# A pre-norm decoder layer on one core: the first tile prepared in halves, three loads reordered, and the loop's pieces placed anew

## What is computed

```python
x = x + self_attention(layernorm(x), Wq, Wk, Wv, Wo)   # 32 heads, 8 key/value heads of 16, RoPE, causal
x = x + cross_attention(layernorm(x), ctx, Wq, bq, Wk, bk)  # softmax((xWq+bq)(ctxWk+bk)^T / sqrt(512)) ctx
h = layernorm(x)                                       # FFN with weights rounded to -1, 0, 1 times a scale
x = x + ((h @ gate.T) * (h @ up.T)) @ down.T           # inner width 1376
```

## Time and profile before

| | us |
|---|---|
| median of 3 runs (226.37 to 226.87) | 226.63 |
| the profiled execution, its own time | 226.21 |
| its span, first to last instruction | 224.5 |
| PE busy in it | 209.5 |
| DVE, ACT, POOL busy in it | 146.9, 124.6, 65.8 |

### The profile page before, as it was taken

The page is one execution under the profiler, slowest core; times in us unless marked ns, Lnnn a source line. Parts: engine busy times, 40 slices in busy tenths (PEclk is TensorE's granted clock), DMA queues, the critical chain, the costliest instruction groups (busy, mean ns, idle before and its releaser), DMA issues.

```text
span 224.5 us, 4343 instructions
## 1 busy us (share of the span) xinstructions
PE 209.5 (93%) x1500; PEld 152.0 (68%) x1500; DVE 146.9 (65%) x556; ACT 124.6 (56%) x210; POOL 65.8 (29%) x87
## 2 busy tenths in 40 slices
PE   8899999999897899998999997999999999999993
PEld 3389878677664675565945445788887877767771
DVE  2488677967889875998424589886645665343333
ACT  2748788777988346197767917357325033323220
POOL 4599917794223383152202212000000010000000
PEclk9999999999999999999999999999999999999999
DMA  6999500024612210649000640000000000020002
GB/s 176 377 402 411 196 1 1 7 72 183 237 65 61 84 49 13 178 134 309 20 4 0 205 170 0 3 0 3 0 0 1 3 0 3 0 93 3 0 0 95
DMA packets 9078, 19.98 MB, mean 89 GB/s; under 512 B 1152, under 2 KB 1536, under 8 KB 9056
## 3 DMA queue, kind: packets, MB, share of 16 engines
q1 hardware_dynamic: 8480, 19.60, 25.2%
q10 hardware_dynamic: 576, 0.10, 0.2%
HBM read 18.58 MB, written 1.05 MB: 87 GB/s over the span
## 4 chain that ended last, share of the span: by engine, by line
PE 77%; DVE 7%; ACT 6%; issue 5%; DMA 3%; SPq 1%; DVEq 0%; POOL 0%; ACTq 0%
PE ps L1376 17%; PE ps L1230 13%; PE ps L1391 8%; PE ps L1267 5%; PE ps L1298 3%; PE ps L1329 3%; PE ps L1210 3%; PE ps L1439 3%; DMA wqkv<-wqkv_dram 3%; PE ps L1164 3%; PE ps L1521 3%; PE ps L1450 2%; PE ps L1480 2%; PE ps L1179 2%; PE ps L1189 2%
## 5 line engine op out<-in xcount | busy, mean ns | idle before, releaser
L1044 DVE CUSTOM_DVE_ANT_0 ps<-ps,maskf 128x128 f32<-128x128 f32 (+1 forms) x128 | 41.2, 394 | 3.4 <-PE ps L1450 2.1
L584 POOL TENSOR_SCALAR_AFFINE_SELECT prob<-prob 128x512 f32<-128x512 f32 x32 | 19.8, 642 | 49.0 <-ACT prob L802 49.0
L802 ACT ACTIVATE prob<-ps 128x1536 f32<-128x1536 f32 x16 | 23.3, 1455 | 19.4 <-PE ps L1486 19.4
L503 POOL TENSOR_TENSOR rstd<-veps,neghalf 128x1 f32<-128x1 f32 x12 | 7.3, 609 | 57.7 <-DVE veps L837 57.7
L672 ACT CAST in_hi<-inter 128x256 f16<-128x256 f32 (+1 forms) x22 | 8.9, 405 | 23.1 <-DVE inter L997 23.1
L1376 PE MATMUL ps<-h_hi,gate_q 128*128 128x256 f16 (+1 forms) x88 | 20.4, 273 | 0.0
L1376 PE MATMUL ps<-h_lo,up_q 128*128 128x256 f16 (+1 forms) x88 | 20.4, 273 | 0.0
L1376 PE MATMUL ps<-h_lo,gate_q 128*128 128x256 f16 (+1 forms) x88 | 20.4, 273 | 0.0
L1376 PE MATMUL ps<-h_hi,up_q 128*128 128x256 f16 (+1 forms) x88 | 20.4, 272 | 0.0
L997 DVE TENSOR_TENSOR inter<-gate_s,ps 128x256 f32<-128x256 f32 (+1 forms) x22 | 9.2, 419 | 15.6 <-PE ps L1376 14.7
L665 ACT ACTIVATE gate_s<-ps 128x256 f32<-128x256 f32 (+1 forms) x22 | 8.4, 384 | 18.8 <-PE ps L1376 18.8
(11 more groups left out here) (189 smaller groups left out, 539.2 us busy)
## 6 DMA issues: line engine op xcount, KB each, us to landing
raw<-gate_dram SPq DMA_DIRECT2D x1, 2752.0 KB, 17.1
raw<-up_dram SPq DMA_DIRECT2D x4, 688.0 KB, 4.1
wqkv<-wqkv_dram SPq DMA_DIRECT2D x4, 384.0 KB, 5.8
raw<-down_dram SPq DMA_DIRECT2D x2, 768.0 KB, 5.2
x<-x_dram SPq DMA_DIRECT2D x4, 256.0 KB, 5.2
xwq<-xwq_dram SPq DMA_DIRECT2D x1, 1024.0 KB, 8.9
xwk<-xwk_dram SPq DMA_DIRECT2D x1, 1024.0 KB, 11.1
wo<-wo_dram SPq DMA_DIRECT2D x1, 1024.0 KB, 18.2
```

Of the source, the lines that this page charges most:

```text
L584: nc.gpsimd.affine_select(out=v, in_=v, compare_op=ALU.is_ge, fill=0.0, base=0, pattern=[[0, GROUP], [1, P]], channel_multiplier=-1).then_ ...
L802: nc.scalar.activation(prob[:, i % 2, :], ps[:, 3:6, :].rearrange("p a b -> p (a b)"), ACT.Exp, scale=DH ** -0.5).then_inc(exp_done, 1)
L1044: nc.vector.tensor_tensor_reduce(scores, scores, mask, 1.0, LOWEST, ALU.add, ALU.max, to).then_inc(max_done, 1)
```

## The change

**The first tile.** DVE normalises tile 0 in two halves of 256 columns. PE transposes each half into a bank of its own (banks 0 and 6) and ACT copies each on its own. `project_first` now takes one part k of the weights and does both column ranges with it, so q, k and v of tile 0 are complete together; the transposes of tile 1 stand ahead of the last part, and ACT copies them ahead of the last high part of the weights. The DVE order of the statistics and of `tile_low(1)` is as it was.

**The first loads.** x of tile 1 is now issued behind part 1 of the weights, x of tile 2 behind part 3.

**The loop.** Many side pieces have moved by a place or a slot; the chunk (2, 1) goes from DVE to POOL; the context loads start one group later, and down load 0 is issued after group 12 in place of 10, load 1 as before.

```diff
-        TILE_BANK = (0, 5, 6, 0)
+        TILE_BANK = (None, 5, 6, 0)
+        FIRST_BANKS = (0, 6)
...
-        POOL_CHUNKS = [(0, 0), (0, 1), (0, 2), (0, 3), (1, 0), (1, 1), (1, 2), (1, 3), (2, 4)]
+        POOL_CHUNKS = [(0, 0), (0, 1), (0, 2), (0, 3), (1, 0), (1, 1), (1, 2), (1, 3), (2, 1), (2, 4)]
...
-            ([("out", 10), ("max", 13)], [("a", 3, 1), ("n2", 1), ("tern", 1, 3)], [("xT", 1, 0), ("xT", 1, 1),
-             ("high", "wo", 0)]),
-            ([("out", 11), ("max", 14), ("abs", 2, 0), ("abs", 2, 1)], [("g", 0, 0), ("g", 0, 1)], [("abs", 2, 2),
-             ("low", "wo", 0), ("abs", 2, 3)]),
...
-            ([("low", "wo", 3), ("out", 14), ("max", 17), ("n3", 0)], [("xo", 1)], [("tern", 2, 1)]),
...
+            ([("out", 10), ("max", 13)], [("a", 3, 1), ("n2", 1)], [("xT", 1, 0), ("xT", 1, 1), ("high", "wo", 0)]),
+            ([("abs", 2, 0), ("max", 14), ("abs", 2, 1), ("out", 11)], [("g", 0, 0), ("abs", 2, 2), ("g", 0, 1)],
+             [("abs", 2, 3)]),
...
+            ([("max", 17), ("out", 14), ("n3", 0), ("low", "wo", 3)], [("xo", 1)], []),
...
-        UP_LOADS, CTX_LOAD, DOWN_LOADS = {3: (0, 1), 4: (2,), 5: (3,)}, 6, {10: (0,), 12: (1,), 13: (2, 3)}
+        UP_LOADS, CTX_LOAD, DOWN_LOADS = {3: (0,), 4: (1, 2), 5: (3,)}, 7, {12: (0, 1), 13: (2, 3)}
...
             for k in range(KD):
                 sp.dma_start(wqkv[:, k, :], wqkv_d[k * P:(k + 1) * P, :]).then_inc(wqkv_in[k], 16)
-                if k < 2:
-                    load_x(1 + k)
+                if k == 1:
+                    load_x(1)
+            load_x(2)
             load_x(3)
...
+            def first_T():
+
+                for half, full, done in ((0, xnT_half_ps, xnT_half), (1, xnT_ps, xnT_sb)):
+                    act.wait_ge(full, 1)
+                    nc.scalar.copy(xnT[:, 2 * half:2 * half + 2, 0:P],
+                                   bank(FIRST_BANKS[half], T).rearrange("p (k q) -> p k q", k=2)).then_inc(done, 1)
...
-            tile_T(0)
+            first_T()
             weights_high(0)
             weights_high(1)
             normalise(1)
             weights_high(2)
+            tile_T(1)
             weights_high(3)
             normalise(2)
-            tile_T(1)
...
                 if t == 0:
-                    normalise(0, lambda: None)
+                    dve.wait_ge(rstd_ready, 1)
+                    for half, ready in ((0, xn_half), (1, xn_ready)):
+                        cols = slice(half * T, (half + 1) * T)
+                        nc.vector.tensor_scalar(xn[:, 0, cols], x[:, 0, cols], mv[:, 0, 0:1], rstd[:, 0:1],
+                                                ALU.subtract, ALU.mult).then_inc(ready, 1)
...
+            def project_first(k):
+
+                pe.wait_ge(xnT_sb if k >= 2 else xnT_half, 1)
+                pe.wait_ge(wqkv_in[k], 16)
+                for e in range(2):
+                    mm = nc.tensor.matmul(qkv_bank(0, e)[:, 0:QKV - D if e else D], xnT[:, k, 0:P],
+                                          wqkv[:, k, HEAD_COLS[e]], start=(k == 0), stop=(k == KD - 1))
+                    if k == KD - 1:
+                        mm.then_inc(qkv_ps, 1)
...
-            tile_T(0)
-            pe.wait_ge(xnT_sb, 1)
-            project_first(qkv_bank(0, 0), 0).then_inc(qkv_ps, 1)
-            tile_T(1)
-            project_first(qkv_bank(0, 1)[:, 0:QKV - D], 1).then_inc(qkv_ps, 1)
+            first_T()
+            for k in range(KD):
+                if k == KD - 1:
+                    tile_T(1)
+                project_first(k)
```

More of the change, by code:

```diff
@@ L307, in decoder_layer @@
-            ([("max", 15), ("out", 12), ("xs", 0), ("low", "wo", 1), ("low", "wo", 2), ("high", "wo", 1)],
-             [("high", "wo", 2), ("part", 2), ("abs", 2, 4)], [("xs", 1), ("xpT", 0)]),
-            ([("out", 13), ("high", "wo", 3), ("max", 16)], [("whole", 2, 0), ("whole", 2, 1)], [("xpT", 1),
-             ("xo", 0), ("tern", 2, 0)]),
-            ([("low", "wo", 3), ("out", 14), ("max", 17), ("n3", 0)], [("xo", 1)], [("tern", 2, 1)]),
-            ([("xT", 2, 0), ("out", 15), ("n3", 1), ("hl", 0), ("max", 18)], [("cc", 2), ("xT", 2, 1),
-             ("whole", 2, 2)], [("hl", 1), ("whole", 2, 3), ("whole", 2, 4), ("tern", 2, 2)]),
-        ]
@@ L315, in decoder_layer @@
[L315 to L322 removed]
+            ([("abs", 0, 1)], [("pq", 3), ("rot", 3, 0), ("st", 10)], [("abs", 0, 2)]),
@@ new lines, in decoder_layer @@
+            ([("abs", 0, 3), ("max", 0)], [("rot", 3, 1), ("pk", 3), ("st", 11), ("st", 12)], [("part", 0),
+             ("hi", 3, 0)]),
+            ([("whole", 0, 0), ("max", 1)], [], [("whole", 0, 1), ("a", 0, 0), ("whole", 0, 2)]),
+            ([("max", 2)], [("st", 13), ("tern", 0, 0)], [("a", 0, 1), ("tern", 0, 1), ("lo", 3, 0)]),
+            ([("max", 3), ("out", 0), ("st", 14)], [("hi", 3, 1)], [("a", 1, 0), ("st", 15), ("whole", 0, 3),
+             ("tern", 0, 2)]),
+            ([("out", 1), ("max", 4)], [("st", 16)], [("tern", 0, 3), ("lo", 3, 1), ("a", 1, 1), ("st", 17)]),
@@ new lines, in decoder_layer @@
+            ([("out", 2), ("max", 5)], [("st", 18)], [("abs", 1, 0), ("st", 19), ("abs", 1, 1)]),
+            ([("out", 3), ("max", 6)], [("a", 2, 0)], [("abs", 1, 2)]),
+            ([("max", 7), ("out", 4)], [], [("abs", 1, 3)]),
+            ([("out", 5), ("u", 0), ("max", 8)], [], [("u", 1)]),
+            ([("whole", 1, 0), ("out", 6), ("part", 1), ("whole", 1, 1), ("max", 9)], [], []),
+            ([("out", 7), ("whole", 1, 2), ("c",), ("max", 10)], [("cc", 0)], [("a", 2, 1)]),
+            ([("max", 11), ("cc", 1), ("out", 8)], [], [("wo", 0), ("tern", 1, 0)]),
@@ new lines, in decoder_layer @@
+            ([("out", 9), ("max", 12), ("n2", 0), ("wo", 1)], [("tern", 1, 1), ("a", 3, 0), ("whole", 1, 3)],
+             [("tern", 1, 2), ("tern", 1, 3)]),
+            ([("out", 10), ("max", 13)], [("a", 3, 1), ("n2", 1)], [("xT", 1, 0), ("xT", 1, 1), ("high", "wo", 0)]),
+            ([("abs", 2, 0), ("max", 14), ("abs", 2, 1), ("out", 11)], [("g", 0, 0), ("abs", 2, 2), ("g", 0, 1)],
+             [("abs", 2, 3)]),
+            ([("max", 15), ("out", 12), ("abs", 2, 4), ("low", "wo", 0), ("xs", 0), ("high", "wo", 1),
+             ("low", "wo", 1)], [("part", 2), ("high", "wo", 2)], [("low", "wo", 2), ("xs", 1), ("xpT", 0)]),
@@ L1168, in tile_T, with first_T @@
                 pe.wait_ge(xn_ready, t + 1)
+                if t == 2:
+                    pe.wait_ge(xnT_sb, 1)
                 if t == 3:
-                    pe.wait_ge(xnT_sb, 1)
+                    pe.wait_ge(xnT_half, 1)
                 transpose_tile(bank(TILE_BANK[t]), xn[:, t % 2, :]).then_inc(xnT_ps, 1)
             HEAD_COLS = (slice(0, D), slice(D, QKV))
-            def project_first(out, e):
-                for k in range(KD):
-                    pe.wait_ge(wqkv_in[k], 16)
-                    mm = nc.tensor.matmul(out, xnT[:, k, 0:P], wqkv[:, k, HEAD_COLS[e]],
-                                          start=(k == 0), stop=(k == KD - 1))
-                return mm
+            def first_T():
+                for half, ready, full in ((0, xn_half, xnT_half_ps), (1, xn_ready, xnT_ps)):
+                    pe.wait_ge(ready, 1)
+                    for j in range(2):
+                        k = 2 * half + j
+                        mm = nc.tensor.transpose(bank(FIRST_BANKS[half])[:, j * P:(j + 1) * P],
+                                                 xn[:, 0, k * P:(k + 1) * P], ident[:, :])
+                    mm.then_inc(full, 1)
+            def project_first(k):
[6 more added lines that the diff above has]
+                        mm.then_inc(qkv_ps, 1)
             def project_high(out, t, e):
```

39 lines of the change are left out of this document (14 added, 25 removed).

## The result

The changed kernel takes 228.45 us (median of 6 runs, 228.35 to 229.81) where the kernel before takes 226.75 beside it on the same chip: a ratio of 1.0084, with a 95% interval of 1.0064 to 1.0104, or 1.9 us. The forecast was 227.7, 1.1 us more than before. The direction held; the size is nearly twice as large by the ratio and 1.6 times by the medians (1.7 us). The median lies at the upper end of the range (228.5); the ratio, taken on the 226.63 that the prediction started from, gives 228.53, just outside it. Ratios here come from the single executions and can differ by 0.1% from the quotient of the two medians. One execution of the kernel before (727.75 us) and one of a later kernel (271.39 us, mean clock 0.756) are left out of all ratios.

The account below looks back on a forecast made before the run. PE, busy 209.5 of 224.5 us at full clock, was taken as the bound. Start +0.68, steps 15 and 16 +0.26 and step 18 +0.21 gave +1.15: 227.36, 227.8 against the median, taken as 227.7 us; range 226.2 to 228.5.

Parts of the forecast that it names:

- Its likeliest case: The whole kernel: slower at 227.7 us, from terms at the start and in the loop summing to +1.15; chance 0.53.
- step 14: In the loop: ternary chunk (1, 3) delays an exponential and one copy by 0.16 us, later copies start earlier; nothing in sum.
- start, to the first product of tile 1: Before the loop: x of tile 2 lands at 10.79, delaying DVE's low part of tile 1; +0.68 us, bounds 0.3 and 0.8.
- steps 15 and 16: In the loop: an abs chunk between two copies PE waits for, partly offset by earlier down loads; +0.26 us.
- step 17: In the loop: the prediction names no term here.
- step 18: In the loop: `wo`'s low part moves behind the normalisation, the root shortens to 0.55, the addition comes later; +0.21 us.
- rival (c): In the loop: the down loads land as late as before; +1.8 us in the whole, 228.4 us; chance 0.10.
- the first steps of the loop: Loop's first part: two exponentials pushed by 0.3 to 0.4 us, transposes change places on PE; costed at nothing.
- all that is behind the loop: After the loop: moved pieces are each ready at least 0.5 us before they are wanted; costed at nothing.
- POOL at the start: Before the loop: POOL's last two low parts of the weights run 14.8 to 18.5; costed at nothing, upper bound 0.1.
- (a): At the start: loads don't queue by bytes, x of tile 2 lands about as before; 225.9 us, chance 0.16.
- (d): At the start: PE's stall of 1.5 us brings back the slow pace, 1.3 us more; 229.0 us, chance 0.04.

Follow-up runs that it names:

- the old loads: The changed kernel with x of tiles 1 and 2 issued behind parts 0 and 1 of the weights, as before: 227.34 us, ratio 1.0042.
- the three pieces back: The kernel before with the loop's new order, except the abs chunk, ternary chunk (1, 3) and fourth low part of `wo` put back: 226.95 us, ratio 1.0010.
- the tables alone: The kernel before with only the loop's new order of side pieces, first tile and first loads as before: 227.63 us, ratio 1.0060.
- the low part first: The changed kernel, new loads kept, with DVE making the low part of tile 1 ahead of the statistics of tile 3: 229.45 us, ratio 1.0137.
- the abs chunk back: The kernel before with the loop's new order, but the down weights' third chunk summed behind both copies g, as before: 227.44 us, ratio 1.0029.
- The tables with both pieces back: The kernel before with the loop's new order, but the abs chunk and ternary chunk (1, 3) put back: 226.95 us, ratio 1.0009.

## Why the prediction was wrong

Its likeliest case was right in direction and in its mechanism for the start; it fell on its sum, +1.15 forecast and 1.9 measured, and one of its steps, step 14, was wrong outright. The terms, forecast against traces:

| | forecast | measured |
|---|---|---|
| start, to the first product of tile 1 | +0.68 | +1.2 between the means of three and five traces |
| step 14 | 0 | +0.42 to +0.44 |
| steps 15 and 16 | +0.26 | +0.57 and +0.87, both with the old loads |
| step 17 | 0 | +0.11 |
| step 18 | +0.21 | +0.16 |

In the times the new start costs 1.2 us with the old tables and 0.5 with the new, and the new tables cost 1.4 us with the old start and 0.7 with the new. Each of these is known to 0.4 to 0.7 us, so the start may have been sized right. For the loop (+0.47 forecast) the traces are clear: 1.28 us with the old start.

**Step 14** is the step that failed outright: "Nothing in sum". It cost 0.43 us. I followed the ternary chunk on ACT, where the first copy came 0.22 us later (0.16 forecast) and the next ones sooner. I didn't follow the exponential's other reader: its mask on POOL, 1.0 us later, falls on the normalisation on DVE, and that takes 0.94 us instead of 0.54. With the chunk back it takes 0.54 again. Two rows of the kernel before warned of it. One I used for step 18, where the root is 0.93 us beside an instruction of DVE and 0.55 alone. The other is this same normalisation in step 19, beside a chunk that POOL scales:

```profile
135.68 0.92 DVE L844 TENSOR_SCALAR xn<-x,mv,rstd 128x512 f32<-128x512 f32 x1 [0.16 <-POOL rstd L503]
```

```profile
135.63 0.69 POOL L424 TENSOR_SCALAR raw<-raw,inv 96x512 f32<-96x512 f32 x1
```

In step 18 the forecast was right: with the low part moved the root took 0.55, with it back 0.92, and the addition lost 0.16. The Trainium skill (GPSIMD Engine Reference, Specifications) names contention of GpSimd with VectorE instructions in a two-port mode as well as with those of two SBUF inputs; the trace agrees for the root, and the long normalisation, which reads one tile, would fall under the first kind, though no row here shows its mode.

**Steps 15 and 16** were mis-sized in the landing: the chunk between the copies costs, as forecast, but "the loads can land together at about 107.8" was wrong. They landed at 108.71 with the old start, so rival (c) describes these steps better, with 0.57 us of PE's time, and 0.87 with the halves, against my 0.26 and its 0.93. The profiled execution of the changed kernel can't show this term: its clock had fallen, the exponential ends at 109.8, ACT has no wait for the loads, and PE's wait is 0.29 us as before. That the two parts together cost less (0.84%) than their sum (1.14%) may come from a loop that starts later against its loads, or from the intervals alone; no run separates these.

**The start** rests on one figure that came from one execution: "x of tile 2 now lands where part 3 landed ... at 10.79". The rule (what is ahead in the queue sets the landing) held, and so did the chain behind it (2.90 us for 2.92). But the landing varies by 1.1 us between traces, and the 13.87 that the term was counted from by 1.0. The kernel before has some slack on DVE there, since two parts of the weights fewer are ahead of x of tile 2; the new order has none. The bound of 0.3 to 0.8 only looked for overlap of transfers, not for another execution.

**Costed at nothing, and right**: the first steps of the loop (27.68 to 98.45 before, 27.73 to 98.47 with the new tables), and all that is behind the loop (136.75 to 197.36 is 60.61 us; 60.56 with the three pieces back). Step 17's 0.11 us, a wait for `ctx_tok` of 0.41 and not 0.30, wasn't foreseen, and its cause wasn't looked for.

**POOL at the start**: its last two low parts ended at 19.19, not 18.5, and PE's low products took 1.71 us where 1.55 is usual; from the first product of tile 1 to the scores it was 14.03 us instead of 13.81. That is 0.2 us against an upper bound of 0.1.

**Rivals.** (a) fell: no trace with the new order has x of tile 2 before 10.7. (d) fell where it stood: PE stood for 1.51, 1.38 and 1.29 us near 14 us, and the clock stayed. But a fall of the clock came true at a place where I hadn't looked, and as a chance, not as a rule. In the profiled execution of the changed kernel, behind the waits of 0.70 and 0.84 us of step 14:

```profile
106.00:107.00 1.00, 0.16 (x4) 0.17 (x3) 0.98 (x2) 0.83 (x2) 0.00 (x0) 1.00 0.95 336
107.00:108.00 1.00, 1.00 (x10) 1.00 (x11) 0.97 (x6) 0.00 (x0) 0.00 (x0) 0.66 1.05 404
108.00:109.00 1.00, 1.00 (x6) 0.78 (x5) 1.00 (x9) 0.66 (x1) 0.00 (x0) 0.50 0.13 47
109.00:110.00 1.00, 1.00 (x7) 1.00 (x6) 1.00 (x6) 0.94 (x2) 0.14 (x1) 0.50 0.12 33
110.00:111.00 1.00, 1.00 (x7) 1.00 (x7) 0.56 (x4) 1.00 (x1) 1.00 (x2) 0.64 0.72 231
111.00:112.00 1.00, 1.00 (x11) 1.00 (x10) 0.00 (x0) 1.00 (x3) 0.08 (x1) 1.00 0.07 14
```

PE is at its lower level, 1.2 GHz (0.50), for some 3.5 us, and from 106.86 to the weighted values at 115.34 it needs 8.48 us, not 6.99: 1.5 us, about what this execution is longer than the others (1.1 to 1.5).

## What to carry to other kernels

An instruction that is moved has to be followed to every reader of what it delays, on every engine: here the late exponential cost nothing on ACT and 0.4 us through a mask on POOL that met a normalisation on DVE. A term that hangs on the landing time of an early load wants the spread of several executions; an order of loads that puts a chain right behind its load takes more of that spread (226.32 to 228.29 us with the new order alone, 225.93 to 227.31 for the kernel before beside it). And where three engines interlock (statistics, roots and low parts, rotations), moving one step forward pays only if nothing queued behind it is next on the path: of the tries to go further, both that put the low part ahead of the last statistics ended slower, one of them in four executions only.

## What the runs showed of the hardware

- **The clock falls in some executions of kernels with two close stalls.** The five kernels with both stalls in step 14 had a mean clock of 0.989 to 0.992 in 7 of 34 executions (the changed one in 1 of 6, the tables alone in 1 of 6, the old loads in none of 6, the low part first in 3 of 4, the abs chunk back in 2 of 12); in the other eight new kernels it was 0.996 or more in all 89 executions that the comparisons count. Three falls were profiled: two directly behind the stalls of step 14, and that of the tables alone at 138 us, behind step 19's stalls of 1.09 and 0.46. The tables with both pieces back have those same two stalls in step 19 and showed no fall in 11 executions, so what else it takes is open. That it is chance within a kernel, and that a single stall of 1.51 us at 14 us left the clock alone, wasn't expected. The Trainium skill (TensorE: Matmul & The Clock Gate, HAM oscillation) has waits of PE put the clock back to half; the level agrees (0.50), and in these traces the length of a single stall doesn't decide it. Which of the two stalls it takes wasn't tried apart.
- **The warm-up varies by execution.** Its eight passes took from 5.15 to 6.42 us in thirteen traces while the granted clock read 1.00 in each of those microseconds, and six passes took 4.84. With the first tile's products right behind it, that is up to 1 us at their start.
- **Early transfers vary.** Between 5 and 6 us the rate was 191 to 315 GB/s in ten traces with the old order of loads and 122 to 246 in four with the new, and 376 to 420 in every microsecond from 8 to 13 us. That the new order itself lowers the early rate isn't shown, as four traces are few.
